# Narrower node panels for the edge groups of a graph layer: 64 and 96 columns in place of 128

## What is computed

```python
dst = (12500 * uniform(200000) ** 2).astype(int32)       # then sorted, src with it
...
deg  = segment_sum(w, col, MEM_LEN) + 2.0
norm = dinv[row] * w * dinv[col]                          # dinv = rsqrt(deg)
msg  = norm[:, None] * xw[row]                            # xw = layernorm(x) @ W
out  = segment_sum(msg, col, MEM_LEN)                     # one sum per destination node
out  = out + (2.0 * dinv * dinv)[:, None] * xw
...
x = x + out;  x = x + experts(layernorm(x))               # top-1 routing, 8 experts, F = 1024
```

## Time and profile before

| | |
|---|---|
| median of 3 runs | 3101.61 us (3097.3 to 3101.98) |
| the profiled execution's own time | 3100.11 us |
| its span, first to last instruction | 3098.6 us |
| PE busy | 2009.9 us (65%) |
| DVE busy | 1172.9 us (38%) |
| ACT busy | 457.6 us (15%) |
| POOL busy | 1850.6 us (60%) |
| mean granted TensorE clock | 0.798 of 2.4 GHz |

### The profile page before, as it was taken

How to read it: one execution, slowest core, us unless ns; L and a number is a source line. 1 busy time by engine, 2 the same in 40 slices (tenths; PEclk the granted TensorE clock), 3 DMA queues, 4 the chain that set the end, 5 groups by cost and what they waited for, 6 DMA issues and landing times. The chain is left out here.

```text
span 3098.6 us, 38408 instructions
## 1 busy us (share of the span) xinstructions
PE 2009.9 (65%) x10840; PEld 1817.4 (59%) x10841; DVE 1172.9 (38%) x3705; ACT 457.6 (15%) x1152; POOL 1850.6 (60%) x1912
## 2 busy tenths in 40 slices
PE   2066555555566655666566666666655979989995
PEld 1045455555555555555555565565555868878875
DVE  8664222223212112343343343343332435434442
ACT  1341111000000000111111111111111212212221
POOL 6757777777777777777777777777741121111113
PEclk7577778777866677888887777777777989989997
DMA  9677555555444433444444444444442221222111
GB/s 234 177 223 204 154 148 146 150 150 144 142 123 130 131 104 105 130 131 138 143 130 137 143 133 134 137 129 128 136 123 97 69 77 49 68 88 78 57 59 33
DMA packets 229857, 388.32 MB, mean 125 GB/s; under 512 B 38937, under 2 KB 139967, under 8 KB 229546
## 3 DMA queue, kind: packets, MB, share of 16 engines
q0 software_dynamic: 92800, 245.57, 27.7%
q1 hardware_dynamic: 119274, 108.41, 11.8%
q10 hardware_dynamic: 17600, 32.15, 3.0%
HBM read 293.85 MB, written 100.43 MB: 127 GB/s over the span
## 5 line engine op out<-in xcount | busy, mean ns | idle before, releaser
L561 POOL DMA_INDIRECT arena<-z_table,arena x1568 | 1519.0, 969 | 497.5 <-issue 460.9
L1645 PE MATMUL bank<-arena 128*128 128x128 f32 x6272 | 1103.0, 349 | 805.9 <-issue 456.0
L1645 PEld LDWEIGHTS bank<-arena 128*128 128x128 f32 x6272 | 1029.8, 257 | 875.3 <-issue 609.7
L1132 DVE TENSOR_TENSOR nodes<-nodes,bank 128x256 f32 x392 | 165.1, 421 | 1336.1 <-PE bank L1645 1317.9
L674 POOL DMA_INDIRECT out<-arena x128 | 127.2, 994 | 630.1 <-DVE arena L1509 548.2
L1795 PE MATMUL bank<-arena 128*128 128x256 f32 (+1 forms) x1472 | 330.3, 384 | 24.4 <-issue 17.6
L1807 PE MATMUL bank<-arena 128*128 128x256 f32 (+1 forms) x1472 | 326.0, 379 | 0.0
L1795 PEld LDWEIGHTS bank<-arena 128*128 128x128 f32 x1472 | 282.7, 196 | 65.5 <-issue 26.9
L1807 PEld LDWEIGHTS bank<-arena 128*128 128x128 f32 (+1 forms) x1472 | 272.6, 187 | 40.1 <-issue 1.0
L1122 DVE TENSOR_TENSOR arena<-iota_b,arena 128x512 f32<-128x512 bf16 x392 | 268.6, 686 | 0.0
L839 ACT ACTIVATE arena<-bank,arena 128x256 f32<-128x256 f32 (+1 forms) x368 | 152.6, 466 | 560.2 <-PE bank L1795 560.2
(11 more groups left out here) (274 smaller groups left out, 1383.7 us busy)
## 6 DMA issues: line engine op xcount, KB each, us to landing
xs<-zeros ACTq DMA_DIRECT2D x122, 257.0 KB
arena<-z_table,arena POOLq DMA_INDIRECT x1568
arena<-xs SPq DMA_DIRECT2D x43, 514.0 KB, 4.0
arena<-in_L_ffn_w SPq DMA_DIRECT2D x16, 1024.0 KB, 7.6
arena<-in_x SPq DMA_DIRECT2D x98, 128.0 KB, 2.7
arena<-in_x SPq DMA_DIRECT2D x24, 512.0 KB, 4.2
out<-arena SPq DMA_DIRECT2D x24, 512.0 KB
nodes<-in_x SPq DMA_DIRECT2D x12, 896.0 KB, 11.9
```

What stands on the lines that cost most here:

```text
L561: nc.gpsimd.indirect_dma_start(gath[:, slot, t, :], None, z_table, bass.IndirectOffsetOnAxis(ap=idx_ring[:, half, s * GT + t:s * GT + t + ...
L1132: nc.vector.tensor_tensor(where, where, agg_bank[j][:, 0:D].rearrange("p (k c) -> p k c", k=KD), ALU.add).then_inc(S["agg_added"], 1)
L1645: last = nc.tensor.matmul(agg_bank[j][:, k * P:(k + 1) * P], gath[:, slot, t, k * P:(k + 1) * P], sel[:, j, t, :], start=(t == 0), stop=(t ...
```

## The change

The panel of a group becomes 64 node columns wide for the groups below 208, and 96 from group 208 on. `select` compares with 64 or 96 columns, `group` multiplies by a moving operand of 64 or 96 columns, `add_group` adds 2×64 or 2×96 columns. The test for a bad group uses the same widths, so that its two operations on all 392 groups become four on 208 and 184. The last turn of four groups before group 208 is written out of its loop, since it adds narrow panels and selects wide ones. Gathering, its order and its rings are as before; so is the number of instructions on PE. The general way keeps 128 columns and gets a name of its own for its selection, in the same memory.

```diff
+    NARROW, WIDE = 64, 96
+    WIDE_FROM = 208
+    WIDTHS = [(0, WIDE_FROM, NARROW), (WIDE_FROM, GROUPS, WIDE)]
+    PANEL = GT * WIDE
...
-        sel = carve([SR, GT, P])
+        sel = carve([SR, PANEL])
...
+        def panel(j, width):
+            return sel[:, j, 0:GT * width].rearrange("p (t c) -> p t c", t=GT)
...
-            then(nc.vector.tensor_scalar(grp_base[:, :], grp_min[:, :], TOP_BASE, None, ALU.min))
+            for a, b, width in WIDTHS:
+                then(nc.vector.tensor_scalar(grp_base[:, a:b], grp_min[:, a:b], float(NW * P - width), None, ALU.min))
             then(nc.vector.tensor_tensor(grp_max[:, :], grp_max[:, :], grp_base[:, :], ALU.subtract))
-            then(nc.vector.tensor_scalar(grp_bad[:, :], grp_max[:, :], float(P), None, ALU.is_ge))
+            for a, b, width in WIDTHS:
+                then(nc.vector.tensor_scalar(grp_bad[:, a:b], grp_max[:, a:b], float(width), None, ALU.is_ge))
...
-            def select(g, j):
-                nc.vector.tensor_tensor(sel[:, j, :, :], iota_b[:, :].unsqueeze(1).to_broadcast([P, GT, P]),
-                                        rel_b[:, bass.ds(g * GT, GT)].unsqueeze(2).to_broadcast([P, GT, P]),
+            def select(g, j, width=NARROW):
+                nc.vector.tensor_tensor(panel(j, width), iota_b[:, 0:width].unsqueeze(1).to_broadcast([P, GT, width]),
+                                        rel_b[:, bass.ds(g * GT, GT)].unsqueeze(2).to_broadcast([P, GT, width]),
                                         ALU.is_equal).then_inc(S["sel_ok"], 1)
...
-                where = agg[:, :, bass.ds(base, P)]
-                nc.vector.tensor_tensor(where, where, agg_bank[j][:, 0:D].rearrange("p (k c) -> p k c", k=KD),
+                where = agg[:, :, bass.ds(base, width)]
+                nc.vector.tensor_tensor(where, where, agg_bank[j][:, 0:KD * width].rearrange("p (k c) -> p k c", k=KD),
...
-            plain_turns(NEAR_ADD, Q0 * GS // SR)
+            plain_turns(NEAR_ADD, WIDE_FROM // SR - 1)
+            plain_turn(WIDE_FROM // SR - 1, WIDE)
...
-                        last = nc.tensor.matmul(agg_bank[j][:, k * P:(k + 1) * P], gath[:, slot, t, k * P:(k + 1) * P],
-                                                sel[:, j, t, :], start=(t == 0), stop=(t == GT - 1))
+                        last = nc.tensor.matmul(agg_bank[j][:, k * width:(k + 1) * width], gath[:, slot, t, k * P:(k + 1) * P],
+                                                panel(j, width)[:, t, :], start=(t == 0), stop=(t == GT - 1))
```

More of the change, by code:

```diff
@@ L37, in build @@
     FAR = 1048576.0
-    TOP_BASE = float((NW - 1) * P)
     HSTEPS = TILES // 16
@@ L78, in build @@
     FB2 = FT // 2
-    assert TW == BW + 2 and STEPS == 2 * (GROUPS // GS)
+    assert WIDE_FROM == Q0 * GS and TW == BW + 2 and STEPS == 2 * (GROUPS // GS)
     assert PC % XSLOTS == 0 and NCH % 2 == 0 and FB2 == 4 and KD == 2
@@ L184, in build @@
         at[0] = here
-        sel = carve([SR, GT, P])
+        sel = carve([SR, PANEL])
+        at[0] = here
+        rep_sel = carve([GT, P])
+        at[0] = here + SR * GT * P
         slots_at = at[0]
@@ L1118, in nearest, with add_group @@
                 dve.sem_inc(S["near_idx_ok"], 1)
-            def select(g, j):
-                nc.vector.tensor_tensor(sel[:, j, :, :], iota_b[:, :].unsqueeze(1).to_broadcast([P, GT, P]),
-                                        rel_b[:, bass.ds(g * GT, GT)].unsqueeze(2).to_broadcast([P, GT, P]),
+            def select(g, j, width=NARROW):
+                nc.vector.tensor_tensor(panel(j, width), iota_b[:, 0:width].unsqueeze(1).to_broadcast([P, GT, width]),
+                                        rel_b[:, bass.ds(g * GT, GT)].unsqueeze(2).to_broadcast([P, GT, width]),
                                         ALU.is_equal).then_inc(S["sel_ok"], 1)
-            def add_group(g, j, first):
-                base = dve.value_load(base_i[0:1, bass.ds(g, 1)], min_val=0, max_val=(NW - 1) * P)
+            def add_group(g, j, first, width=NARROW):
+                base = dve.value_load(base_i[0:1, bass.ds(g, 1)], min_val=0, max_val=NW * P - width)
                 if not first:
@@ L1164, in _, with plain_turn @@
             nearest()
+            def plain_turn(q, ahead=NARROW):
+                for j in range(SR):
+                    add_group(q * SR + j, j, False)
+                    select(q * SR + (j + SR), j, ahead)
             def plain_turns(a, b):
                 with dve.Fori(a, b) as q:
-                    for j in range(SR):
-                        add_group(q * SR + j, j, False)
-                        select(q * SR + (j + SR), j)
+                    plain_turn(q)
             plain_turns(KNN_STEPS * 16 // SR, NEAR_ADD)
@@ L1286, in _ @@
                 for i in range(GS):
-                    add_group(g0 + i, i % SR, False)
+                    add_group(g0 + i, i % SR, False, WIDE)
                     if g0 + i + SR < GROUPS:
-                        select(g0 + i + SR, i % SR)
+                        select(g0 + i + SR, i % SR, WIDE)
                     if i == 1:
@@ L1328, in _ @@
                         dve.wait_ge(S["rep_relok"], g * NW + (w + 1))
-                        nc.vector.tensor_tensor(sel[:, 0, :, :], iota_b[:, :].unsqueeze(1).to_broadcast([P, GT, P]),
+                        nc.vector.tensor_tensor(rep_sel, iota_b[:, :].unsqueeze(1).to_broadcast([P, GT, P]),
                                                 rep_rel[:, :].unsqueeze(2).to_broadcast([P, GT, P]),
@@ L1634, in chosen_rows, with group @@
                 nc.tensor.transpose(bank[4][:, 0:NE * FT], b1_rows[0:NE * FT, :], ident[0:NE * FT, 0:NE * FT]).then_inc(S["b1_ps"], 1)
-            def group(g, q, slot, first):
+            def group(g, q, slot, first, width=NARROW):
                 j = slot % SR
@@ L1708, in slot_turn @@
                 for slot in range(GS):
-                    group(q * GS + slot, q, slot, False)
+                    group(q * GS + slot, q, slot, False, WIDE)
                     if slot == 0:
@@ L1741, in _ @@
                                 last = nc.tensor.matmul(bank[0][:, k * P:(k + 1) * P], rep_gath[:, t, k * P:(k + 1) * P],
-                                                        sel[:, 0, t, :], start=(t == 0), stop=(t == GT - 1))
+                                                        rep_sel[:, t, :], start=(t == 0), stop=(t == GT - 1))
                         last.then_inc(S["rep_ps"], 1)
```

## The result

The changed kernel takes 3078.11 us (median of four runs, 3075.72 to 3081.36), the kernel before beside it 3101.12 us (3097.3 to 3101.98): a ratio of 0.9929 with a 95% interval of 0.9912 to 0.9946. It is 23.0 us faster, and inside the range of 3077 to 3097, 1.1 us above its lower end; 3084.3 was forecast. The profiled execution after is the slowest of its four, 3081.36 us with a span of 3079.8 us, so the spans differ by 18.8 us and not by 23.

What follows compares the result with a forecast made beforehand. POOL's unbroken beat of 1568 gather DMAs was taken as the bound, with selects delaying it. Hold-ups −17.4, add −0.1, bases +0.2 sum to −17.3 us, from 3101.6 to 3084.3 us; range 3077 to 3097.

Steps and rivals of the forecast that it cites:

- the rule: Gather: a select starting before a DMA delays it by the select's end less the DMA's start less 0.13 us; 28.9 us total.
- The old phases with new lengths: Shorter selects laid on the old trace's timing: narrow hold up 21 DMAs for 2.8 us, wide 39 for 8.7.
- The slide's ends: Selects slid over a whole POOL beat: remaining hold-ups 7.4 to 22.4 us, bounding the saving at 21.5 and 6.5 us.
- a sign that I was wrong: Gather: a median of line 561 other than 949 ns would count against the prediction.
- the hold-ups' term: Gather: shorter selects save 10.4 us in narrow groups and 7.0 us in wide ones, together 17.4 us.
- more than forecast: Kind phases leave 7.4 us of hold-ups and shorter streams also help the tail: 3079 us; chance 0.07.
- PE stays at the low clock: Gather's granted clock may fall to 0.5; the tail begins cold, costing about 4 us: 3088 us; chance 0.13.
- The cover that the prediction named: Gather: POOL's beat of four DMAs, 5.0 us, covers a group's matmuls, 1.9 to 3.8 us, at either clock.
- The selects meet more often: Phases lock so every select comes first: 56.6 us of delays, 3129 us; slower from a 51% hit share; chance 0.06.
- The hold-up doesn't shrink: Gather: delay hangs on a select's presence, not length, or something else takes over; stays at 3101.6 us; chance 0.08.
- A group doesn't fit: A group exceeds its 64- or 96-column panel, so the general way runs, costing some ms; chance 0.01.

Runs made afterwards that it cites:

- The last three runs: On a fourth chip: kernel before unchanged (3102.34 us in its profiled run), and select's column numbers in PSUM with 128 columns (0.9907) and with 64 and 96 (0.9905).
- The rerun: The changed kernel once more, unchanged, on a chip where PE stands still in episodes; ratio 0.995 to the kernel before.
- PSUM kernel with 128 columns: Kernel before with the select's column numbers in PSUM, 128 columns kept; ratios 0.9894 and 0.9903 on chips with standstills, 0.9907 on the fourth chip.
- second profile: Kernel before, unchanged, profiled again on the fourth chip, which has no standstills; 3102.34 us in the profiled run.
- The PSUM kernels: Select's column numbers in PSUM: kernel before with 128 columns (0.9907 on the fourth chip), changed kernel with 64 and 96 columns (0.9905 there).

## Why the prediction was right

**The bound.** As read: POOL's beat, which waits for nobody, sets the end of the gather. The last three runs show that a microsecond of hold-up there moves the last gather by a microsecond (27.9 for 28.3); the medians moved by 31.3 and 30.8 us, which agrees within their intervals.

**The hold-up and its cause.** The step on which everything rested, shown: in every profile with two SBUF inputs the rule gives the sum of the delays to within 0.4 us, the narrow select alone brings them down, the narrow matmul and add alone do not, and one operand in PSUM takes them away at full length. The kernel before has a control in its own trace: its adds, with one SBUF input and one in PSUM, meet 73 gathers in the same way. By the rule that would be 10.0 us; it is −0.1. One of them, where the add ends 0.29 us after the DMA's start:

```profile
884.92 0.42 DVE L1132 TENSOR_TENSOR nodes<-nodes,bank 128x256 f32 x1 [2.24 <-PE bank L1645]
885.05 0.94 POOL L561 DMA_INDIRECT arena<-z_table,arena  x1 [0.30 <-issue]
```

The prediction called the 28.9 us nearly the whole excess of 31.0. That takes in 1.9 us of sends, which the 31.0 do not hold: selects are 27.0 of it, distances 3.1. The Trainium skill ("SBUF — State Buffer", section "Who interferes with whom") says that a DVE instruction with at most one SBUF input, outside the two-port modes, does not contend with GpSimd; the traces agree, with 0.1 us over 190 meetings. Its inference that descriptor generation is not disturbed by a tensor_tensor stands against 28.9 us here; for these indirect DMAs the measurement decides.

**The sizes.** Select lengths came out at 418 and 551 ns (median; 416 and 550 forecast), the add at 289 and 355 (290 and 350). The old phases with new lengths gave 2.8 us for narrow selects and 8.7 for wide; measured 2.2 and 10.1. Together 12.3 against 11.5. The rerun, on a chip with standstills, had 10.4, so some 2 us of such a sum can be the execution's own. The slide's ends of 7.4 and 22.4 us were both far off; the phases stay kinder than random.

**What the forecast lacked.** 6.2 us at the median. Between the two profiled executions 0.8 us less came from the hold-ups than forecast, 1.3 was lost at start and tail, and 3.6 us were gained in the rest of the gather: 1.5 more in all. The 3.6 us go with a median DMA of 946 in place of 949 ns, which I had called unchanged and whose change I had listed as a sign that I was wrong. It is not the change's: the same changed kernel shows 949 on another chip, the same PSUM kernel with 128 columns 949 once and 946 twice. A beat repeated 1568 times turns a difference of 3 ns between executions into 4.7 us. The other 4.7 us lie between a profiled execution and the median of its runs: the forecast had put +1.5 us there, from the runs of before, where after has −3.3. So the hold-ups' term was right to 0.8 us, and the rest of the distance is spread that nobody forecast. It brought the time to within 1 us of the 3079 of *more than forecast*, whose two conditions did not come true (the hold-ups are 12.3 us and not 7.4, and the tail is no shorter); that it still fell inside the range, by 1.1 us, has some luck in it.

**The matmuls.** PE gained nothing from 64 columns, as forecast. Sixteen weight loads take 3.49 us at the lower clock with 64 and with 96 moving columns, and 1.86 at the full clock with 96, both as with 128 in the earlier trace rows; the tail's last group takes 3.70 us, and the 24 matmuls after it 7.21 where they took 7.14:

```profile
482.94 3.49 PEld L1660 LDWEIGHTS bank<-arena 128*128 128x128 f32 x16 [1.51 <-DVE arena L1133]
...
1237.28 1.86 PEld L1660 LDWEIGHTS bank<-arena 128*128 128x128 f32 x16 [0.82 <-issue]
...
2249.33 3.49 PEld L1660 LDWEIGHTS bank<-arena 128*128 128x128 f32 x16 [3.45 <-issue]
...
2271.56 3.70 PE L1660 MATMUL bank<-arena 128*128 128x96 f32 x16 [2.81 <-issue]
...
2279.47 7.21 PE L1687 MATMUL bank<-arena,nodes 128*128 128x256 f32 x24
```

The kernel before in its second profile has 2.61 and 7.70 us in the same two places, so a tenth or half a microsecond there is chance. The rule of about 60 cycles for 64 columns (the Trainium skill, "TensorE: Matmul & The Clock Gate", section "Back-to-back issue gap", which states it for a matmul by itself and not for a stream of weight loads and matmuls) would by an estimate have given up to 1 us; the trace does not have it. The tail's group is no test of that rule by itself, since it has 96 columns and ran at the lower clock; what speaks against the rule for this stream of weight load and matmul are the 0.11 us at the full clock, the same with 8, 96 and 128 columns. Groups of 64 columns got the full clock too seldom in this trace to be read there.

**The rivals.** *PE stays at the low clock* had its premise come true (0.52 and 0.69 in the gather) but not its price: the tail after the last gather is 813.5 us against 812.9, not 4 us longer. The tail did begin at the lower clock, but the granted clock rises during its 24 matmuls (columns as in the windows above; the stretches before, at and behind these matmuls):

```profile
2268.00:2279.00 11.00, 4.87 (x22) 4.41 (x22) 3.61 (x19) 1.51 (x2) 0.00 (x0) 0.50 0.43 76
2279.00:2284.00 5.00, 5.00 (x17) 4.18 (x17) 2.75 (x15) 0.00 (x0) 0.96 (x1) 0.59 0.94 340
2284.00:2290.00 6.00, 2.68 (x13) 2.02 (x11) 4.20 (x14) 0.00 (x0) 3.03 (x4) 0.99 0.70 243
```

In the kernel before the clock was 0.66, 0.64 and 0.95 at the same three places: it fell and rose there too. The cover that the prediction named held: POOL waits for PE at most 0.3 us. *The selects meet more often*: a share of 65 in 392, where 51% would have been needed. *The hold-up doesn't shrink* is refuted. *A group doesn't fit* did not occur. *More than forecast* came close in time without its reasons, as said above.

## What stays open

Why PE stands still at multiples of 0.70 us on three of the chips (of the kernel before only the time, 760 us longer, speaks for it there, as it was not profiled on them). How much of a hold-up reaches the time on them: 5.5 and 11.5 us for 23 and 33.5 us of hold-ups between kernels on one chip, but these pairs are few. And why, on them, the kernels with 128-column matmuls (granted clock 0.70 to 0.71; 0.9937, 0.9894, 0.9903, 0.9924) come out below those with 64 and 96 (0.64; 0.995, 0.9956, 0.9953): the granted clock is higher with them, but that this is the reason was only argued. Whether the PSUM kernels beat the change where PE does not stand still was not compared on one chip; the ratios 0.9905 and 0.9907 against 0.9929 have overlapping intervals, and the hold-ups that the change leaves, 12.3 us, are 0.4% of its time. On one of the chips with standstills the comparison is direct: 0.9894 for PSUM with 128 columns against 0.995 for the change, with intervals apart.

## What to carry to other kernels

Where GpSimd issues indirect DMAs back to back and is the bound, look at their durations' excess over the median before their count: each DVE instruction with two SBUF inputs (here tensor_tensor and scalar_tensor_tensor) that starts just before one holds it up until about its own end. Put one of the operands in PSUM, split the instruction, or make it shorter; the first removed all of it for two small copies and one bank less in the rotation of the group sums, and left the panels as they were. An engine off the path can thus cost time with no wait in the profile naming it, and to test such a reading one edit that changes the cause without changing the length is worth more than several that change both.

## What the hardware showed that was not expected

- The same program on different chips takes 3101 to 3106 us or 3860 to 3868. In the latter PE issues one weight load or matmul at a time, at multiples of 0.70 us, in 34 to 45 episodes of up to 34 us.
- Halving the moving columns at an unchanged pace of weight loads (3.49 us for 16) took the granted clock from 0.76 to 0.52 in the first stage, with PE's busy time there up from 624.8 to 783.7 us. The PSUM kernels on the fourth chip show it again: 0.78 there with 128 columns, 0.52 with 64. A kernel can lose its clock by an edit that removes work; here it cost nothing.
- The indirect DMA takes 946 to 949 ns (median); the same program has 946 in one execution and 949 in another.
